# Weight splits off GpSimd, finer waits before scores and the output projection, and in seven of sixteen Runge-Kutta stages the square of q on ScalarE

## The chip, the cores and the metric

One core of one Trainium2 chip runs the whole kernel. The metric is the device time of one execution in microseconds (us), taken as the median over runs; lower is better. Engines are named PE (TensorE), DVE (VectorE), ACT (ScalarE), POOL (GpSimd) and SP (SyncE, which issues the transfers).

## The reference

Inputs are x (32 x 32 x 256) and a condition of 32 x 256. Two blocks follow each other.

- First block: `x = x + minGRU(DiT(x, cond))`. DiT is a layer norm with a condition-dependent scale and shift, attention with 16 heads of 128 over 32 tokens, a gated output projection and residual, a second such norm and a GELU MLP of width 1024. minGRU is a gated linear recurrence over the 32 tokens.
- Second block: `x = x + FFN(scan(cond, x))`. The scan runs 32 time steps, each a classical Runge-Kutta step of four stages; FFN is a block-sparse MLP that keeps 4 of 16 hidden blocks for each row. The scan's derivative is what the change touches most:

```python
def _derivative(q, p, drive, coupling, bias):
    i_couple = jnp.tanh(q) @ coupling.T
    dq = q - q ** 3 / 3.0 - p + drive + i_couple + bias
    dp = EPSILON * (q + ALPHA - BETA * p)
    return (dq, dp)
```

Step t needs the result of step t-1, so its 32 x 4 = 128 stages form one chain.

## The kernel before

Every engine has its program written out by hand, with semaphores between them; nothing is scheduled by a planner. Matrix products run in fp16 in three parts: an operand is split into a high part (fp16 of 16 times the value) and a low part (what is left), and high x high, high x low and low x high are summed.

**Start and four attention passes.** The layer norm and `x1` come first (`drive`, then `x1_pair`). Then four passes of four heads each (`for i in range(NQUAD)`). In a pass PE runs, for heads j = 0 to 3, `project(j)` (q and k), `values`, `scores(j)`, `mix(j)` (probabilities times values) and `out_project`, through five PSUM banks; a bank used again waits until DVE has emptied it. ACT copies each bank to its high part (`high`), DVE subtracts to the low part and frees the bank (`low_proj`, `low_values`, `low_pv`), DVE adds the output projections into `acc` (`add_heads`), and DVE, ACT and POOL make the softmax and place it in block-diagonal form (`shift`, `exps`, `normalise`, `place_high`, `place_low`). Eight pieces of weights per pass are split: ACT writes the high part (L528), POOL scales the weights in place (L473) and subtracts (L475), and SP loads the next pass's piece when that is done (`split_ready`).

**Waits on PE in a pass.** `taken(use)` waits until a bank has been emptied. `scores(j)` (L850) waits for both the last projections' banks before its first product; `out_project` with c = 0 (L883) waits for both halves of each head's `mix`.

**The last pass and the middle.** In the last pass ACT and POOL also split the first eight pieces of MLP weights (L550, then POOL L464 and L466). DVE gates the heads and adds the residual (`close_heads`, L1201 and L1203, three of four before `low_pv(3)`), adds the last heads (`last_heads`, L1212 and L1215), takes mean and variance (`token_var`) and finishes the square root that ACT begins (`root_x2` on ACT, `token_scale` on DVE). Then `modulate`, `x1_low`, and PE's `hidden_layer(0)`, `output_layer(0)`, `hidden_layer(1)`, `gates(0)`, `output_layer(1)`, `gates(1)`, with the minGRU on DVE.

**The scan.** 32 steps in eight groups of four, so a group has 16 stages, numbered `at` = 0 to 15. A stage is

1. ACT: `th16` = tanh(q) in fp16 (L754), then `th32` = tanh(q) in fp32 (L755), then scalings of p or pieces of the FFN (L732, L740, L745);
2. DVE: `sq` = q*q (L1499), `cub` = (sq + c)*q (L1505), `thlo` = th32 - th16 (L1495, which waits for th32), `base` (L1511), and running sums for later stages (`lin` L1603, `pacc` L1613) between them;
3. PE: the drive, then th16 x two coupling parts (8 matmuls), then thlo x one coupling part (4 matmuls), then pieces of the previous group's FFN (`FILL`);
4. DVE: `qs` or `qn` = score*h + base (L1517), which starts the next stage.

`group_work(n, at, slot)` puts DVE's share of the FFN into slot 0 (behind thlo) or slot 1 (before L1517): `split_h` (L1543), the top-4 selection, `split_q` (L1587) and `put_out` (L1552, from the third group on). In a stage whose `at` is a multiple of 4 (s = 0), thlo stands ahead of cub.

## Time and profile before

| | us |
|---|---|
| median of 3 runs | 533.71 (532.94 to 535.42) |
| the profiled execution | 534.34 |
| its span, first to last instruction | 532.6 |
| start and first pass, to 81.4 | 81.4 |
| second and third pass | 57.35 and 56.95 |
| last pass and its end, 195.7 to 273 | 77.3 |
| MLP and minGRU, 273 to 343.7 | 70.7 |
| scan, 343.7 to 521 | 177.3 |
| end, 521 to 532.6 | 11.6 |

Over the span PE is busy 454.7 us, DVE 418.1, ACT 319.1 and POOL 179.6. A share of busy time is an average over very different parts: in the scan DVE is busy 174.05 of 177.30 us, in the third pass 36.22 of 56.95. A busy time on DVE includes the latency of an instruction, and the next one may start before it ends, so the distances between starts say more than the busy times.

### The profile page before, as it was taken

How to read it: one execution, taken by the hardware profiler on the slowest of the kernel's cores; microseconds unless marked ns; L12 is line 12 of the kernel's file. 1: busy time of each engine (PE TensorE's matmuls, PEld its weight loads, DVE VectorE, ACT ScalarE, POOL GpSimd, SP SyncE). 2: the span in 40 equal slices, each digit the busy share in tenths (PEclk: the TensorE clock that was granted, in tenths of full speed). 3: DMA queues.
4: the chain of work that ended last, by engine and by line, in shares of the span. 5: the costliest groups of instructions: out<-in, count | busy, mean ns of one | idle time of the engine just before them, and what ended most of it. 6: DMA issues, size and time to landing. Idle time of an engine off the chain costs nothing.

```text
span 532.6 us, 13455 instructions
## 1 busy us (share of the span) xinstructions
PE 454.7 (85%) x4832; PEld 312.3 (59%) x4832; DVE 418.1 (79%) x1632; ACT 319.1 (60%) x881; POOL 179.6 (34%) x173
## 2 busy tenths in 40 slices
PE   2999789998999989987569998398887888879886
PEld 2555576456655665556425443286776767767676
DVE  4968765668566666577886786999999999999994
ACT  1377763787477746896258763555656556565563
POOL 4528347563737363879800890000000000000000
PEclk9899899999999999999769999777979788797799
DMA  8961502020112000000000000000000000000000
GB/s 304 414 268 38 124 1 80 17 62 1 24 55 62 17 0 0 0 1 0 0 0 1 1 2 0 0 4 1 0 1 12 1 10 10 0 10 1 10 10 21
DMA packets 10127, 20.82 MB, mean 39 GB/s; under 512 B 1456, under 2 KB 4720, under 8 KB 9456
## 3 DMA queue, kind: packets, MB, share of 16 engines
q1 hardware_dynamic: 9536, 19.89, 11.1%
q10 hardware_dynamic: 560, 0.60, 0.3%
q8 instruction: 10, 0.16, 0.1%
q14 instruction: 21, 0.17, 0.1%
HBM read 19.40 MB, written 1.08 MB: 38 GB/s over the span
## 4 chain that ended last, share of the span: by engine, by line
DVE 47%; PE 33%; ACT 10%; issue 6%; DMA 1%; POOL 1%; SPq 0%; DVEq 0%; ACTq 0%
PE bank L791 26%; DVE base L1511 5%; PE score L791 5%; DVE lin L1603 5%; DVE qs L1517 4%; DVE cub L1505 3%; DVE big L1284 3%; DVE sq L1499 3%; DVE pacc L1613 2%; ACT sraw L586 2%; ACT ao_sb L561 1%; DVE thlo L1495 1%; DVE ao_sb L1284 1%; DVE big L1543 1%; DMA ao_sb<-xtok 1%
## 5 line engine op out<-in xcount | busy, mean ns | idle before, releaser
L791 PE MATMUL bank<-x,pairs_store 128*128 128x512 f16 x384 | 87.8, 386 | 0.0
L482 POOL TENSOR_TENSOR ptx<-pt,ptx 32x256 f16<-32x256 f32 x64 | 42.8, 668 | 71.0 <-ACT ptx L593 67.3
L791 PE MATMUL score<-th,coup_part 128*128 128x32 f16 x1024 | 48.1, 182 | 18.9 <-ACT th L754 16.3
L791 PEld LDWEIGHTS bank<-x,pairs_store 128*128 128x128 f16 x384 | 37.9, 100 | 44.3 <-issue 3.0
L561 ACT ACTIVATE big<-bank,pass_b 128x512 f16<-128x512 f32 x64 | 42.8, 685 | 28.5 <-PE bank L791 26.5
L791 PE MATMUL bank<-pairs_store,ao_sb 128*128 128x256 f16 x384 | 48.6, 283 | 10.5 <-DVE ao_sb L1284 9.9
L791 PEld LDWEIGHTS score<-th,coup_part 128*128 128x128 f16 x1024 | 36.4, 100 | 30.4 <-ACT th L754 29.1
L754 ACT ACTIVATE th<-qs 128x64 f16<-128x64 f32 x96 | 24.4, 254 | 49.7 <-DVE qs L1517 49.7
L1284 DVE SCALAR_TENSOR_TENSOR big<-bank,pass_b,big 128x512 f16<-128x512 f32 x64 | 44.9, 741 | 11.6 <-ACT big L561 11.6
L791 PEld LDWEIGHTS bank<-pairs_store,ao_sb 128*128 128x128 f16 x384 | 37.5, 101 | 19.4 <-DVE ao_sb L1284 10.2
L791 PE MATMUL bank<-pairs_store,x 128*128 128x512 f16 x192 | 43.4, 379 | 0.0
L791 PE MATMUL score<-drive_pair,scaled_eye 128*128 x256 | 32.3, 209 | 11.9 <-DVE drive_pair L1446 8.9
L791 PE MATMUL bank<-big,f_sb 128*128 128x128 f16 x456 | 39.8, 232 | 0.2 <-DVE big L1543 0.2
L791 PE MATMUL bank<-q_high,f_sb 128*128 128x128 f16 x288 | 39.3, 251 | 0.0
L791 PE MATMUL score<-thlo,coup_part 128*128 128x32 f16 x512 | 34.8, 183 | 3.6
L791 PEld LDWEIGHTS score<-drive_pair,scaled_eye 128*128 128x128 f16 x256 | 25.2, 120 | 14.2 <-issue 13.9
L791 PE MATMUL bank<-q_low,f_sb 128*128 128x128 f16 x144 | 33.5, 252 | 0.0
L1282 DVE TENSOR_TENSOR big<-bank,big 128x512 f16<-128x512 f32 x32 | 21.5, 682 | 14.4 <-ACT big L559 14.4
L473 POOL TENSOR_SCALAR wqk_sb<-wqk_sb 128x512 f32<-128x512 f32 x16 | 23.8, 1489 | 23.8 <-ACT pairs_store L528 23.1
L791 PE MATMUL score<-big 128*128 128x128 f16 x384 | 25.2, 224 | 7.6 <-DVE big L1284 7.6
L791 PEld LDWEIGHTS bank<-pairs_store,x 128*128 128x128 f16 x192 | 18.6, 98 | 21.7
L732 ACT ACTIVATE pscaled<-ps 128x64 f32<-128x64 f32 x160 | 29.9, 243 | 0.4 <-DVE ps L1621 0.4
(196 smaller groups left out, 1133.1 us busy)
## 6 DMA issues: line engine op xcount, KB each, us to landing
wqk_sb<-wqk SPq DMA_DIRECT2D x16, 256.0 KB, 2.7
wv_sb<-wv SPq DMA_DIRECT2D x4, 512.0 KB, 5.3
wo_sb<-wo SPq DMA_DIRECT2D x4, 512.0 KB, 3.7
f_sb<-ffn_w SPq DMA_DIRECT2D x2, 1024.0 KB, 14.4
ao_sb<-xtok SPq DMA_DIRECT2D x4, 256.0 KB, 5.6
big<-ada_w SPq DMA_DIRECT2D x1, 1024.0 KB, 9.1
x_sb<-xT SPq DMA_DIRECT2D x1, 1024.0 KB, 13.1
w_sb<-w1T SPq DMA_DIRECT2D x1, 1024.0 KB, 16.8
```

The source lines that it names most:

```text
L473: nc.gpsimd.tensor_scalar(w, w, WSCALE, None, ALU.mult).then_inc(pool_scaled, 1)
L482: nc.gpsimd.tensor_tensor(ptx[s, 1, :, s], pt[s], ptx[s, 0, :, s], ALU.subtract).then_inc(ptx_ready, 1)
L561: ins = nc.scalar.activation(dst, src, ACT.Identity, bias=bias)
L732: nc.scalar.activation(pscaled[:, j], ps[:], ACT.Copy, scale=PSCALE[j]).then_inc(p_scaled, 1)
L754: nc.scalar.activation(th16[:], src, ACT.Tanh).then_inc(th16_ready, 1)
L791: return nc.tensor.matmul(dst, lhsT, rhs, start=start, stop=stop, **kw)
L1282: ins = V.tensor_tensor(lo, bank[bank_of(use)][:], hi, ALU.subtract)
L1284: ins = V.scalar_tensor_tensor(lo, bank[bank_of(use)][:], bias, hi, ALU.add, ALU.subtract)
L1499: squared = mark(V.tensor_tensor(kb(sq[:]), q, q, ALU.mult))
L1511: based = mark(stt(base[:], cub[:], -STAGE_H[s] / 3.0, linear, ALU.mult, ALU.add))
L1517: stt(qs[:, s] if s < 3 else qn[:], kb(score[:, s % 2, 0:KB * B]), STAGE_H[s] / CSCALE, kb(base[:]), ALU.mult, ALU.add).then_inc(q_ready, 1)
L1603: lined[n] = mark(stt(kb(lin[:, n]), q, row, src, ALU.mult, ALU.add))
```

## The change

1. **Splits.** POOL no longer splits weights. DVE writes each low part in one instruction, `w*16 - high`, with nothing scaled in place: piece 0 ahead of the first `drive` products, pieces 1 to 3 behind `x1`, then in each pass pieces 4 to 7 among the low parts and pieces 0 to 3 of the next pass between the last `add_heads`. The 16 MLP pieces go to DVE too: 0 to 3 ahead of `shift(3)` in the last pass, 4 to 7 and 12 to 15 among the hidden layer's low parts, 8 to 11 before `residual(0)`. POOL keeps `place_low`.
2. **Waits on PE.** `scores(j)` waits for its first two banks before product 0 and for the other two before product 4. `out_project` waits for the first half of `mix` at c = 0 and for the second at c = 2.
3. **Second norm.** `close_heads(2)` moves behind `token_scale(0)`, `close_heads(3)` behind `x1_low(0)`. The root of the second half is made by DVE alone (an integer seed and three Newton steps); ACT takes one root and loads the GELU table at once.
4. **Scan.** In the stages 7, 9, 10, 11, 13, 14 and 15 of each group ACT squares q behind th32, DVE's `sq` goes, and DVE runs thlo and the FFN piece ahead of cub.

```diff
+        SQUARE_AT = (7, 9, 10, 11, 13, 14, 15)
...
-                for t in range(NSPLIT):
-                    split(t)
-                    if t == 3:
...
+                place_low(0)
+                pool.wait_ge(ptx_ready, i * (QUAD * NB4) + NB4)
...
+            act.wait_ge(tok_var_ready, 1 + G // 2)
+            nc.scalar.activation(tok_std[:, 0:G // 2], tok_mv[:, 0:G // 2, 1], ACT.Sqrt, bias=eps[:]).then_inc(tok_std_ready, 1)
+            nc.scalar.activation(eps_gelu[:], eps[:], ACT.Gelu)
...
                     nc.scalar.activation(th32[:], src, ACT.Tanh).then_inc(th32_ready, 1)
+                    if n in SQUARE_AT:
+                        nc.scalar.activation(square_q[:], src, ACT.Square).then_inc(squared_ready, 1)
...
                 def scores(j):
-                    taken(USE_PROJ[j] + 2)
-                    taken(USE_PROJ[j] + 3)
...
                     for g in range(G):
+                        if g % 4 == 0:
+                            taken(USE_PROJ[j] + g // 2)
+                            taken(USE_PROJ[j] + g // 2 + 1)
...
+                    if c % 2 == 0:
+                        for j in js:
+                            taken(USE_PV[j] + c // 2)
...
+                def low_weights(i, *ts):
+                    for t in ts:
+                        w, pair = split_arrays(*SPLIT_ORDER[t])
+                        dve.wait_ge(w_high_ready, i * NSPLIT + t + 1)
+                        V.scalar_tensor_tensor(pair[:, 1], w, WSCALE, pair[:, 0], ALU.mult, ALU.subtract
+                                               ).then_inc(split_ready, 1)
...
                 low_pv(1)
+                if i == NQUAD - 1:
+                    mlp_lows(0, 1, 2, 3)
                 shift(3)
...
                     for c in range(KB * NH):
+                        low_weights(i + 1, c)
                         add_heads(1, c)
...
-                squared = mark(V.tensor_tensor(kb(sq[:]), q, q, ALU.mult))
+                at = 4 * (t % UNROLL) + s
+                by_act = at in SQUARE_AT
+                if not by_act:
+                    squared = mark(V.tensor_tensor(kb(sq[:]), q, q, ALU.mult))
                 if second:
                     second()
                 if late:
                     low(t, s)
-                dve.wait_ge(dve_step, squared)
-                cubed = mark(stt(kb(cub[:]), kb(sq[:]), -3.0 - 3.0 * own_q / STAGE_H[s], q, ALU.add, ALU.mult))
-                if not late:
+                if by_act:
+                    group_work(t // UNROLL, at, 0)
+                    low(t, s)
+                    group_work(t // UNROLL, at, 1)
+                    dve.wait_ge(squared_ready, len(SQUARE_AT) * (t // UNROLL) + SQUARE_AT.index(at) + 1)
+                else:
+                    dve.wait_ge(dve_step, squared)
+                cubed = mark(stt(kb(cub[:]), kb((square_q if by_act else sq)[:]), -3.0 - 3.0 * own_q / STAGE_H[s], q,
+                                 ALU.add, ALU.mult))
+                if not late and not by_act:
                     low(t, s)
                 ready()
-                group_work(t // UNROLL, 4 * (t % UNROLL) + s, 0)
+                if not by_act:
+                    group_work(t // UNROLL, at, 0)
                 dve.wait_ge(dve_step, cubed)
                 based = mark(stt(base[:], cub[:], -STAGE_H[s] / 3.0, linear, ALU.mult, ALU.add))
                 if third:
                     third()
-                group_work(t // UNROLL, 4 * (t % UNROLL) + s, 1)
+                if not by_act:
+                    group_work(t // UNROLL, at, 1)
```

How the order on DVE moves in stage 10, a scan stage with a `put_out`. Names: `lin` are the running sums, `x<-bank,drive` is the `put_out`, `square_q` is ACT's square. Before:

```order
L1603 SCALAR_TENSOR_TENSOR lin<-qs,lin 128x64
L1499 TENSOR_TENSOR sq<-qs 128x64
L1603 SCALAR_TENSOR_TENSOR lin<-qs,lin 128x64
L1505 SCALAR_TENSOR_TENSOR cub<-sq,qs 128x64
L1495 TENSOR_TENSOR thlo<-th 128x64
L1511 SCALAR_TENSOR_TENSOR base<-cub,lin 128x64
L1603 SCALAR_TENSOR_TENSOR lin<-qs,lin 128x64
L1552 SCALAR_TENSOR_TENSOR x<-bank,drive 128x128
L1517 SCALAR_TENSOR_TENSOR qs<-score,base 128x64
```

The same stage in the changed kernel:

```order
L1641 SCALAR_TENSOR_TENSOR lin<-qs,lin 128x64 x2
L1521 TENSOR_TENSOR thlo<-th 128x64
L1590 SCALAR_TENSOR_TENSOR x<-bank,drive 128x128
L1540 SCALAR_TENSOR_TENSOR cub<-square_q,qs 128x64
L1548 SCALAR_TENSOR_TENSOR base<-cub,lin 128x64
L1641 SCALAR_TENSOR_TENSOR lin<-qs,lin 128x64
L1555 SCALAR_TENSOR_TENSOR qs<-score,base 128x64
```

Before, cub stands ahead of thlo and the FFN piece last, between base and qs. Now thlo and the piece stand ahead of cub, and cub, base, lin and qs follow them.

The end of the last pass on DVE, before, from the second half of `add_heads` to the variance. L1201 and L1203 are `close_heads`, L1284 is `low_pv(3)`, L1212 and L1215 `last_heads`:

```order
L1332 TENSOR_TENSOR acc<-bank,acc 128x512
L1201 TENSOR_TENSOR acc<-acc,drive 128x512
L1203 TENSOR_TENSOR acc<-acc,centred 128x512
L1201 TENSOR_TENSOR acc<-acc,drive 128x512
L1203 TENSOR_TENSOR acc<-acc,centred 128x512
L1201 TENSOR_TENSOR acc<-acc,drive 128x512
L1203 TENSOR_TENSOR acc<-acc,square 128x512
L1284 SCALAR_TENSOR_TENSOR ao_sb<-bank,pass_b,ao_sb 128x512 x2
L1212 TENSOR_TENSOR nn_<-bank,drive 128x512
```

The same place in the changed kernel (L1187 and L1189 are `close_heads`, L1283 `low_pv(3)`):

```order
L1338 TENSOR_TENSOR acc<-bank,acc 128x512
L1187 TENSOR_TENSOR acc<-acc,drive 128x512
L1189 TENSOR_TENSOR acc<-acc,centred 128x512
L1187 TENSOR_TENSOR acc<-acc,drive 128x512
L1189 TENSOR_TENSOR acc<-acc,centred 128x512
L1283 SCALAR_TENSOR_TENSOR ao_sb<-bank,pass_b,ao_sb 128x512 x2
L1198 TENSOR_TENSOR nn_<-bank,drive 128x512
```

One `close_heads` of three has left the place ahead of `low_pv(3)`.

## Rows read from the trace of the kernel before

**Rows 1.** Stretches: us, busy per engine (instructions), granted PE clock, DMA share, GB/s
```profile
343.70:521.00 177.30, 151.54 (x2657) 127.52 (x2657) 174.05 (x1168) 101.11 (x467) 0.00 (x0) 0.84 0.02 5
```
**Rows 2.** Timeline, one stage (14) of the sixth group: start, us, engine, line, tiles
```profile
451.29 0.23 DVE L1517 SCALAR_TENSOR_TENSOR qs<-score,base 128x64 f32<-128x64 f32 x1
...
451.71 0.24 ACT L755 ACTIVATE th<-qs 128x64 f32<-128x64 f32 x1
...
451.99 0.23 DVE L1495 TENSOR_TENSOR thlo<-th 128x64 f16<-128x64 f32 x1
...
452.27 0.26 PE L791 MATMUL score<-thlo,coup_part 128*128 128x32 f16 x4
...
452.64 0.23 DVE L1517 SCALAR_TENSOR_TENSOR qs<-score,base 128x64 f32<-128x64 f32 x1
```
**Rows 3.** Timeline, DVE, stage 9 with its put_out
```profile
444.33 0.22 DVE L1517 SCALAR_TENSOR_TENSOR qs<-score,base 128x64 f32<-128x64 f32 x1
...
445.47 0.37 DVE L1552 SCALAR_TENSOR_TENSOR x<-bank,drive 128x128 f32<-128x128 f32 x1
445.76 0.22 DVE L1517 SCALAR_TENSOR_TENSOR qs<-score,base 128x64 f32<-128x64 f32 x1
```
**Rows 4.** Timeline, DVE, a stage with at = 0: thlo to cub to base
```profile
432.56 0.23 DVE L1495 TENSOR_TENSOR thlo<-th 128x64 f16<-128x64 f32 x1
432.71 0.22 DVE L1505 SCALAR_TENSOR_TENSOR cub<-sq,q_group 128x64 f32<-128x64 f32 x1
...
432.98 0.22 DVE L1511 SCALAR_TENSOR_TENSOR base<-cub,pscaled 128x64 f32<-128x64 f32 x1
```
**Rows 5.** Timeline, DVE: a 128-wide piece to qs; base to qs with nothing between
```profile
457.94 0.28 DVE L1587 TENSOR_TENSOR q_low<-q_group,q_high 128x128 f16<-128x128 f32 x1
458.17 0.23 DVE L1517 SCALAR_TENSOR_TENSOR qs<-score,base 128x64 f32<-128x64 f32 x1
...
466.14 0.23 DVE L1511 SCALAR_TENSOR_TENSOR base<-cub,pscaled 128x64 f32<-128x64 f32 x1
466.40 0.22 DVE L1517 SCALAR_TENSOR_TENSOR qs<-score,base 128x64 f32<-128x64 f32 x1
```
**Rows 6.** Waits of PE in the second and third pass: us in total, times, longest
```profile
PE score L791 <- DVE big L1284: 3.9, 4, 1.3
PE bank L791 <- DVE ao_sb L1284: 3.0, 4, 1.1
```
**Rows 7.** Timeline, end of the third pass
```profile
188.03 2.87 POOL L482 TENSOR_TENSOR ptx<-pt,ptx 32x256 f16<-32x256 f32 x4 [3.62 <-ACT ptx L593]
...
194.12 4.39 PE L791 MATMUL bank<-pairs_store,ao_sb 128*128 128x256 f16 x36 [0.35 <-DVE ao_sb L1284]
```
**Rows 8.** Timeline, end of the last pass and the second norm
```profile
242.45 0.42 DVE L1295 TENSOR_REDUCE smax<-sraw 128x8 f32<-128x256 f32 x1 [2.62 <-ACT sraw L586]
...
251.47 1.65 DVE L1201 TENSOR_TENSOR acc<-acc,drive 128x512 f32<-128x512 f32 x1
...
254.06 1.40 DVE L1284 SCALAR_TENSOR_TENSOR ao_sb<-bank,pass_b,ao_sb 128x512 f16<-128x512 f32 x2
255.60 6.98 PE L791 MATMUL bank<-pairs_store,ao_sb 128*128 128x256 f16 x36 [3.46 <-DVE ao_sb L1284]
...
273.16 13.21 PE L791 MATMUL bank<-x,wqk_sb 128*128 128x512 f16 x48 [4.97 <-issue]
```
**Rows 9.** L1201 in all (ns min/median/max), then DVE groups, 247.8 to 263: busy us, mean ns
```profile
L1201 DVE TENSOR_TENSOR acc<-acc,drive x4: 684/992/1651, 247.8 to 265.5; 128x512 f32<-128x512 f32 x4
...
L1203 DVE TENSOR_TENSOR acc<-acc,centred 128x512 f32<-128x512 f32 x2 | 1.7, 868 | 0.1
L1215 DVE TENSOR_TENSOR acc<-acc,tn 128x512 f32<-128x512 f32 x1 | 1.7, 1660 | 0.1
...
L1215 DVE TENSOR_TENSOR acc<-acc,nn_ 128x512 f32<-128x512 f32 x1 | 1.2, 1204 | 0.1
```
**Rows 10.** Timeline, ACT's switch to another table before the MLP
```profile
275.99 1.28 ACT L680 ACT_TABLE_LOAD   x1
```

More of the change, by code:

```diff
@@ L19 @@
 BF16 = mybir.dt.bfloat16
+I32 = mybir.dt.int32
+ROOT_SEED = 0x5F3759DF
 AX_X = mybir.AxisListType.X
@@ L678, in _ @@
             x1_high(NH)
-            root_x2(1)
-            nc.scalar.activation(eps_log[:], eps[:], ACT.Gelu)
             for h in range(NH):
@@ L1168, in _ @@
                 last.then_inc(x1_ready, 1)
+            first_low_weights(1, 2, 3)
             def late_start():
@@ L1184, in _, with mlp_lows @@
             ln = Own(dve, ln_step)
+            def mlp_lows(*ts):
+                for t in ts:
+                    w, high_part, low_part = mlp_arrays(t)
+                    dve.wait_ge(mlp_high_ready, t + 1)
+                    V.scalar_tensor_tensor(low_part, w, WSCALE, high_part, ALU.mult, ALU.subtract).then_inc(mlp_split, 1)
             def pair_of(c):
@@ L1228, in token_scale @@
                 gs = slice(h * G // 2, (h + 1) * G // 2)
-                dve.wait_ge(tok_std_ready, h + 2)
-                ln.step(V.reciprocal(tok_rstd[:, gs], tok_std[:, gs]))
-                ln.wait()
-                ln.step(V.tensor_tensor(tok_tmp[:, gs], tok_rstd[:, gs], tok_rstd[:, gs], ALU.mult))
-                ln.wait()
-                ln.step(V.scalar_tensor_tensor(tok_tmp[:, gs], tok_mv[:, gs, 1], LN_EPS, tok_tmp[:, gs], ALU.add, ALU.mult))
-                ln.wait()
-                ln.step(V.tensor_scalar(tok_tmp[:, gs], tok_tmp[:, gs], -0.5, 1.5, ALU.mult, ALU.add))
-                ln.wait()
-                ln.step(V.tensor_tensor(tok_rstd[:, gs], tok_tmp[:, gs], tok_rstd[:, gs], ALU.mult))
+                if h == 0:
+                    dve.wait_ge(tok_std_ready, 2)
+                    ln.step(V.reciprocal(tok_rstd[:, gs], tok_std[:, gs]))
+                    steps = 1
+                else:
+                    dve.wait_ge(tok_var_ready, 1 + G)
+                    ln.step(V.tensor_scalar(tok_std[:, gs], tok_mv[:, gs, 1], LN_EPS, None, ALU.add))
+                    ln.wait()
+                    ln.step(V.tensor_scalar(tok_tmp[:, gs].bitcast(I32), tok_std[:, gs].bitcast(I32), 1, None,
+                                            ALU.arith_shift_right))
+                    ln.wait()
+                    ln.step(V.tensor_scalar(tok_rstd[:, gs].bitcast(I32), tok_tmp[:, gs].bitcast(I32), -1, ROOT_SEED,
+                                            ALU.mult, ALU.add))
+                    steps = 3
+                for _ in range(steps):
+                    ln.wait()
+                    ln.step(V.tensor_tensor(tok_tmp[:, gs], tok_rstd[:, gs], tok_rstd[:, gs], ALU.mult))
+                    ln.wait()
+                    ln.step(V.scalar_tensor_tensor(tok_tmp[:, gs], tok_mv[:, gs, 1], LN_EPS, tok_tmp[:, gs], ALU.add, ALU.mult))
+                    ln.wait()
+                    ln.step(V.tensor_scalar(tok_tmp[:, gs], tok_tmp[:, gs], -0.5, 1.5, ALU.mult, ALU.add))
+                    ln.wait()
+                    ln.step(V.tensor_tensor(tok_rstd[:, gs], tok_tmp[:, gs], tok_rstd[:, gs], ALU.mult))
                 ln.wait()
@@ L1316, in low_projs @@
                         low_proj(j, k)
+                def low_weights(i, *ts):
+                    for t in ts:
+                        w, pair = split_arrays(*SPLIT_ORDER[t])
+                        dve.wait_ge(w_high_ready, i * NSPLIT + t + 1)
+                        V.scalar_tensor_tensor(pair[:, 1], w, WSCALE, pair[:, 0], ALU.mult, ALU.subtract
+                                               ).then_inc(split_ready, 1)
                 def low_values(*gs):
@@ L1338, in _ @@
                 normalise(0)
-                low_values(3, 4, 5)
-                low_projs(1)
+                low_values(3, 4)
+                low_weights(i, 4)
+                low_values(5)
+                low_proj(1, 0)
+                low_proj(1, 1)
+                low_weights(i, 5)
+                low_proj(1, 2)
+                low_proj(1, 3)
+                low_weights(i, 6)
                 if i == 0:
@@ L1345, in _ @@
                 normalise(1)
-                low_projs(2)
+                low_proj(2, 0)
+                low_proj(2, 1)
+                low_weights(i, 7)
+                low_proj(2, 2)
+                low_proj(2, 3)
                 low_pv(0)
@@ L1361, in _ @@
                     for c in range(KB * NH):
+                        low_weights(i + 1, c)
                         add_heads(1, c)
                 else:
-                    for c in range(3):
-                        close_heads(c)
+                    close_heads(0)
+                    close_heads(1)
                     low_pv(3)
@@ L1371, in _ @@
                     token_scale(0)
-                    close_heads(3)
+                    close_heads(2)
                     last_heads(2)
@@ L1378, in _ @@
             x1_low(0)
+            close_heads(3)
             last_heads(3)
```

49 lines of the change are left out of this document (13 added, 36 removed).

## Prediction

> **What bounds the kernel now.** I read the stretches first, then the timeline of single stages, then PE's waits, then the end of the last pass. The sum is made against the profiled execution, 534.34 us, which is 0.6 above the median of 533.71.
>
> The scan takes 177.3 of 532.6 us, and DVE is busy 174.05 of it [rows 1]; a stage lasts 177.3 / 128 = 1.39 us. The timeline shows why the busy share alone says little. In stage 14 q comes at 451.29, th32 runs on ACT from 451.71 to 451.95, thlo starts on DVE at 451.99, its matmuls on PE at 452.27 (0.26 long), and the next q at 452.64, 0.11 behind their end [rows 2]. That is a closed loop of 1.35 us, q to th32 to thlo to PE to q. In it thlo cannot start before q + 0.70, because it waits for th32, whatever DVE does. DVE fills the same 1.35 us with sq, cub, base and sums, most of them in the 0.70 us ahead of thlo. So the stage has two chains of nearly the same length, and the question is what stands ahead of thlo and what behind it.
>
> In the second and third pass PE waits 3.9 + 3.0 = 6.9 us on DVE [rows 6], 3.5 a pass. From the last pass to the MLP, PE sits idle 3.46 us before 255.60, and `hidden_layer(0)` starts at 273.16 [rows 8]. From there PE runs nearly without a break to 334, so what moves that start moves the rest.
>
> **The scan: 56 stages.** Removed: sq on DVE. Added: a square on ACT behind th32. An ACT instruction of this size takes 0.24, as th32 does [rows 2]; it starts some 0.15 behind th32's start, so it ends at q + 0.42 + 0.15 + 0.24 = 0.81. ACT's later pieces in these stages move by 0.15, and have the rest of the stage as cover; without it the next th16 would be late by as much.
>
> Moved: cub now comes behind thlo and the FFN piece. None of the seven stages has a piece in slot 0, so between the sums and thlo DVE has nothing to do: thlo stays at q + 0.70, and the slot that sq leaves is idle time. Behind thlo a chain begins that formerly ran ahead of it:
>
> - thlo to the FFN piece: +0.15 (thlo to cub, 432.56 to 432.71 [rows 4]);
> - a 128-wide piece to cub: +0.20 (0.23 to qs with one more wait instruction between [rows 5]; 0.03 off for that);
> - cub to base: +0.27 (432.71 to 432.98 [rows 4]), since base reads cub;
> - base to q: between 0.26 with nothing in between [rows 5] and 0.32 with a `lin` of 0.14 and two waits; taken 0.29.
>
> Sum: 0.70 + 0.15 + 0.20 + 0.27 + 0.29 = 1.61 against 1.35, so +0.26 in stages 7, 11, 13, 14 and 15. The square, ready at 0.81, is waited for by nobody, and the coupling on PE, ready at 1.24, isn't either: the FFN piece, cub and base end last. Bounds per stage: +0.18 (the shortest of each distance, a piece of 0.17) and +0.33 (a longer base to q, an extra wait instruction at cub).
>
> Stages 9 and 10 carry a `put_out`, 0.29 to the next instruction, and last 1.43 now (444.33 to 445.76 [rows 3]). After: 0.70 + 0.15 + 0.29 + 0.27 + 0.29 = 1.70, +0.27. In the first two groups they have no `put_out`: 0.70 + 0.15 + 0.27 + 0.29 = 1.41 against 1.35, +0.06.
>
> Over the scan: 5 x 8 x 0.26 = 10.4, 2 x 6 x 0.27 = 3.2, 2 x 2 x 0.06 = 0.2: **+13.8 us**, between +9.5 and +17.
>
> **The passes.** DVE takes 8 splits a pass at 0.69 each (an instruction of 128x512 with two SBUF inputs, minimum 0.684 [rows 9]), 5.5 us. Most lie where DVE waits for ACT. Three places are on PE's path. (1) Piece 7 stands ahead of the last two `low_proj(2)`: it takes back what the finer wait at `scores(2)` gives. (2) `scores(3)` starts some 0.7 sooner, but ACT's copy of the scores is queued behind `place_high(2)`, and `mix(3)` waits for the last ptx, made on POOL from 188.03 to 190.90 after a wait on ACT of 3.62 [rows 7]. The wait moves ahead of `mix(3)` and stays. (3) Piece 0 of the next pass stands ahead of the `add_heads` whose bank PE needs: +0.69, less the 0.35 before 194.12 [rows 7] that the finer wait saves: +0.3. For three pass ends +0.9. In the first pass three early pieces stand behind x1, and three more among late work: +0.4. Bounds: -3 (half of PE's waits gone) and +4 (piece 0 in full, and one split a pass more on the path).
>
> **The end of the last pass.** `close_heads(2)` leaves the path: 251.47 to 254.06, -2.6 [rows 8]. DVE no longer meets POOL's scalings: L1201 0.992 twice and L1203 0.868 twice against 0.684, L1215 1.66 and 1.20 against 0.69 [rows 9]: 0.62 + 0.37 + 0.97 + 0.51 = -2.5. Against it, MLP pieces 0 to 3 ahead of `shift(3)`: 4 x 0.69 = 2.76 in a wait of 2.62 [rows 8], and some 0.4 for meeting POOL's ptx there: +0.55. Together **-4.6**. Bounds: -7 (PE at full clock in `hidden_layer(0)`, which takes 13.21 for the 48 matmuls [rows 8]) and -2.
>
> The Trainium skill's SBUF — State Buffer (the section that explains the port diagram) says that DVE and GpSimd share one port pair as an exclusive lock, and that the loser blocks for the whole instruction. By it each of the four pieces could wait for a whole ptx instruction of 0.72, 2.9 us in place of 0.4, and the time would be 2.5 higher. L1201's average excess of 0.31 to 0.97 is nearer to a part of an instruction.
>
> Priced at nothing: the two table loads (ACT then runs ahead of PE's first hidden tile; if uncovered 1.3 [rows 10]); the DVE square root of the second half, ten small instructions of 0.2 under 13.21 us of PE, and if late, `turn_normed(1)` is late; MLP pieces 4 to 15 under PE's matmuls; the next weights' loads, many us ahead.
>
> **Sum.** 534.34 + 13.8 + 0.9 + 0.4 - 4.6 = 544.8; on the scale of the medians **544.2 us**.
>
> **The rivals.**
>
> 1. *The scan is a count of DVE's instructions, and one less is a gain* (ends on the other side). For it: DVE busy at 98%, and stages with `put_out` last longer. Then each of 56 stages loses one slot of 0.135, -7.6, and with the front's -3.3 the time is 522.8. It decides if thlo can start before q + 0.70 or the piece and cub fit beside it. Against it: thlo starts 0.04 behind th32's end [rows 2] with sq in place or not. Chance 0.05.
> 2. *PE's waits in the passes really vanish* (half of 3.5 or more in four passes, and a full clock at the MLP, -9 in all beyond mine): 535. ptx [rows 7] speaks against it. Chance 0.06.
> 3. *The passes become bound by DVE*: one or two splits a pass more on the path, 4 x 1.2: 549. Chance 0.08.
> 4. *ACT must load tables for Square*. One load takes 1.28 [rows 10]; two per stage, 112 x 1.28 = 143: 687. The built program has no load near the squares. Chance 0.01. The Trainium skill, ScalarE: Activation LUTs (Table sets), says that functions come in sets, that a switch costs about 2.66 us, and doesn't name square under the GELU set; by its figure it would be twice that.
> 5. The forecast, 0.80.
>
> **How the numbers follow.** A measurement tells 0.5%, about 2.7 us, from no change: same is 531.0 to 536.4. Faster is rival 1 and a small part of 2: 0.07. Same is most of 2 and the cheap ends of mine (9.5 with -8 in front gives 535): 0.06. Slower 0.87. The range takes the scan's +9.5 with -6 in front, 537, to +17 with -1.5, 549, and so most of rival 3.
>
> **What would show it.** In the changed kernel's seven stages: thlo at q + 0.70, the piece 0.15 behind it, cub 0.2 behind that, and base to q without a wait on PE; DVE's busy time in the scan lower although the scan is longer; PE's wait for ACT's th16 longer in these stages. Scan about 191 us, `hidden_layer(0)` at about 270 us. Wrong would be: thlo ahead of q + 0.6, these stages at 1.4 or less, or passes off 57 us by more than 1.

## The result, and the profile after

The changed kernel takes 539.22 us (median of 5 runs, 538.80 to 541.05) against 533.90 (5 runs beside it): the ratio is 1.0097, 95% interval 1.0069 to 1.0126. It is slower by about 1%. The forecast was 544.2 us, range 537 to 549, with 0.87 on slower; so 10.5 us were forecast over the 533.71 of the record, and 5.3 came. The profiled execution is the slowest of the five, 541.05 us, span 539.3.

First the stretches of the changed kernel: start, us, busy time of PE, PE's weight loads, DVE, ACT, POOL (instructions), granted PE clock, DMA share, GB/s.

```profile
334.34:527.20 192.86, 160.06 (x2667) 133.85 (x2668) 174.84 (x1119) 109.60 (x523) 0.00 (x0) 0.77 0.02 5
133.46:190.32 56.86, 53.14 (x432) 34.03 (x432) 40.59 (x76) 38.52 (x77) 10.95 (x16) 1.00 0.12 37
```

The first line runs 2 us past the last q. From the first scan matmul to the end of the last q, DVE is busy 173.76 of 176.98 us before (1166 instructions) and 173.25 of 191.04 in the changed kernel (1110). So 14 us were added, and 56 squares less took only 0.5 us off DVE's busy time, because instructions that stand further apart overlap less: in the run e3 below, which has all 1166 in the new order, they cover 178.99 us. The busy share fell from 98% to 91%, and the stage is still DVE's to end. The third pass (second line) has DVE busy 40.59 us where it was 36.22, and takes no longer.

One stage of the seven, at = 14, in the timeline (start, us, engine, line, tiles, idle time before and its releaser):

```profile
425.57 0.22 DVE L1555 SCALAR_TENSOR_TENSOR qs<-score,base 128x64 f32<-128x64 f32 x1
...
426.13 0.24 ACT L722 ACTIVATE square_q<-qs 128x64 f32<-128x64 f32 x1
...
426.25 0.22 DVE L1521 TENSOR_TENSOR thlo<-th 128x64 f16<-128x64 f32 x1 [0.20 <-ACT th L720]
426.39 0.28 DVE L1581 TENSOR_TENSOR big<-big 128x128 f16<-128x128 f32 x1
426.53 0.29 PE L758 MATMUL score<-thlo,coup_part 128*128 128x32 f16 x4
426.60 0.22 DVE L1540 SCALAR_TENSOR_TENSOR cub<-square_q,qs 128x64 f32<-128x64 f32 x1
...
426.92 0.23 DVE L1548 SCALAR_TENSOR_TENSOR base<-cub,lin 128x64 f32<-128x64 f32 x1
427.06 0.22 DVE L1641 SCALAR_TENSOR_TENSOR lin<-qs,lin 128x64 f32<-128x64 f32 x1
427.20 0.22 DVE L1555 SCALAR_TENSOR_TENSOR qs<-score,base 128x64 f32<-128x64 f32 x1
```

Read it against [rows 2]. thlo still starts 0.68 behind q, now with 0.20 of idle time ahead of it. Behind it come the FFN piece (+0.14), cub (+0.21), base (+0.32), a running sum and the next q (+0.28): 1.63 us instead of 1.35. PE's coupling is done at 426.82, 0.38 ahead of q; before it was 0.11 ahead.

Stage 9, with a `put_out`, on DVE alone, against [rows 3]:

```profile
417.36 0.22 DVE L1555 SCALAR_TENSOR_TENSOR qs<-score,base 128x64 f32<-128x64 f32 x1
...
418.06 0.22 DVE L1521 TENSOR_TENSOR thlo<-th 128x64 f16<-128x64 f32 x1 [0.21 <-ACT th L720]
418.20 0.36 DVE L1590 SCALAR_TENSOR_TENSOR x<-bank,drive 128x128 f32<-128x128 f32 x1
418.48 0.22 DVE L1540 SCALAR_TENSOR_TENSOR cub<-square_q,qs 128x64 f32<-128x64 f32 x1
418.80 0.23 DVE L1548 SCALAR_TENSOR_TENSOR base<-cub,lin 128x64 f32<-128x64 f32 x1
...
419.08 0.22 DVE L1555 SCALAR_TENSOR_TENSOR qs<-score,base 128x64 f32<-128x64 f32 x1
```

Outside the scan, the edge of a pass against [rows 7]:

```profile
127.15 1.48 PE L758 MATMUL bank<-pairs_store,ao_sb 128*128 128x256 f16 x12 [1.30 <-DVE ao_sb L1283]
129.32 1.51 PE L758 MATMUL bank<-ptx,big 128*128 128x128 f16 x24 [0.69 <-POOL ptx L470]
...
134.29 1.91 PE L758 MATMUL bank<-pairs_store,ao_sb 128*128 128x256 f16 x16 [0.83 <-DVE acc L1338]
```

The wait on POOL's ptx has moved ahead of the mix (0.69), and the last line shows a new one: 0.83 us for DVE's addition, behind the next pass's first weight piece.

To compare many runs I cut each profiled execution at PE's instructions: first projection, first projection of each later pass, first FFN matmul, first matmul of the scan, and DVE's last q. In us:

| kernel | to first projection | first pass | second, third pass | last pass and its end | MLP, minGRU | scan | behind it |
|---|---|---|---|---|---|---|---|
| before | 21.9 | 62.1 | 57.3, 57.0 | 74.8 | 70.6 | 176.8 | 12.1 |
| before, scan part added (e2) | 22.4 | 59.7 | 57.3, 57.0 | 73.3 | 70.4 | 191.4 | 15.2 |
| changed | 20.8 | 59.3 | 56.9, 56.9 | 69.6 | 71.0 | 190.8 | 14.1 |
| changed, scan part undone (e1) | 19.7 | 58.8 | 56.9, 56.9 | 69.4 | 70.9 | 177.0 | 13.7 |

The first two run the same program as far as the scan, and so do the last two. Within each pair the difference is the scatter of one execution: up to 1.1 us to the first projection, 2.4 in the first pass, 1.5 in the last, next to nothing in between.

### The profile page after: what moved, and what is told of

It is laid out like the page before. It is cut to its first block, busy times and chain, and to the rows that moved or that the text cites. A ratio compares the mean times of both kernels' runs of the same rounds, so it can differ in the third digit from the quotient of the medians.

```text
span 539.3 us, 13473 instructions
## 1 busy us (share of the span) xinstructions
PE 458.9 (85%) x4832; PEld 317.9 (59%) x4832; DVE 431.0 (80%) x1634; ACT 327.2 (61%) x936; POOL 48.7 (9%) x77
## 4 chain that ended last, share of the span: by engine, by line
DVE 43%; PE 33%; ACT 13%; issue 6%; POOL 2%; DMA 1%; DVEq 0%; ACTq 0%
PE bank L758 29%; DVE lin L1641 4%; DVE pacc L1651 3%; DVE base L1548 3%; DVE cub L1540 3%; DVE thlo L1521 3%; DVE qs L1555 3%; DVE big L1283 2%; PE score L758 2%; POOL ptx L470 2%; ACT th L720 2%; ACT sraw L557 2%; DVE big L1581 2%; ACT ptx L564 2%; PE spare L758 2%
## 5 line engine op out<-in xcount | busy, mean ns | idle before, releaser
L470 POOL TENSOR_TENSOR ptx<-pt,ptx 32x256 f16<-32x256 f32 x64 | 44.8, 700 | 195.4 <-ACT ptx L564 191.8
L758 PE MATMUL bank<-pairs_store,ao_sb 128*128 128x256 f16 x384 | 46.1, 275 | 9.7 <-DVE ao_sb L1283 6.4
L1283 DVE SCALAR_TENSOR_TENSOR big<-bank,pass_b,big 128x512 f16<-128x512 f32 x64 | 45.1, 738 | 9.2 <-ACT big L532 9.1
L758 PE MATMUL bank<-big,f_sb 128*128 128x128 f16 x456 | 46.5, 258 | 0.2 <-DVE big L1581 0.2
L758 PE MATMUL bank<-q_high,f_sb 128*128 128x128 f16 x288 | 37.4, 243 | 0.0
L758 PEld LDWEIGHTS bank<-big,f_sb 128*128 128x128 f16 x456 | 34.2, 115 | 0.5 <-issue 0.3
L1521 DVE TENSOR_TENSOR thlo<-th 128x64 f16<-128x64 f32 x128 | 28.7, 225 | 6.9 <-ACT th L720 6.7
L758 PE MATMUL bank<-q_low,f_sb 128*128 128x128 f16 x144 | 32.1, 245 | 0.0
L758 PEld LDWEIGHTS score<-thlo,coup_part 128*128 128x128 f16 x512 | 22.2, 101 | 14.3
```

Of the source, the lines that this page charges most:

```text
L470: nc.gpsimd.tensor_tensor(ptx[s, 1, :, s], pt[s], ptx[s, 0, :, s], ALU.subtract).then_inc(ptx_ready, 1)
L758: return nc.tensor.matmul(dst, lhsT, rhs, start=start, stop=stop, **kw)
L1283: ins = V.scalar_tensor_tensor(lo, bank[bank_of(use)][:], bias, hi, ALU.add, ALU.subtract)
L1521: V.tensor_tensor(thlo[:], th32[:], th16[:], ALU.subtract).then_inc(lo_ready, 1)
```

## The experiments

### The scan part, taken out and put in alone

`e1_scan_undone` is the changed kernel with

```
-        SQUARE_AT = (7, 9, 10, 11, 13, 14, 15)
+        SQUARE_AT = ()
```

> The changed kernel with an empty list of stages for ScalarE's square, so every stage runs as before; the rest of the change (low parts on VectorE, the order at the pass edges, the finer TensorE waits) stays. Theory A (the seven stages cost the time and nothing else in the scan changed; the part ahead of the scan gained 9.4 us by its first matmul, 343.73 to 334.34): scan back from about 193 to 178.7 us, first scan matmul unchanged at 334.3, median 539.2 - 14.1 = 525, so 0.983 of the kernel before. Rival B (part of the stages' cost belongs to the fewer POOL operations or to another part of the change): scan stays above 181, median above 528.

Measured: 524.92 us (524.41 to 526.71, 5 runs), ratio to before 0.9855, 0.9831 to 0.9879. `e2_scan_alone` is the kernel before with ScalarE's square and the new order of these stages, nothing else.

> The kernel before with only the scan part of the change. Theory A (the parts are additive, the seven stages alone cost 14 us): first scan matmul at 343.7 as before, scan 192.9, median 533.9 + 14.1 = 548, so 1.026. Rival B (the stages' cost depends on how the rest was rearranged): less than 1.02.

Measured: 549.28 us, ratio 1.0307, 1.0268 to 1.0347. Both ways the seven stages cost 14 to 16 us by the medians, and the scan went from 177 to 191 us (e2's profile also has 15.2 us behind the scan, see the last section). Theory A holds. It also follows that the rest of the change gains some 8 us, and that the version without the scan part is faster than either kernel.

### What in the stage costs the time

`e3_vector_square` keeps the change's order, but VectorE squares:

```
-                if not by_act:
-                    squared = mark(V.tensor_tensor(kb(sq[:]), q, q, ALU.mult))
+                squared = mark(V.tensor_tensor(kb(sq[:]), q, q, ALU.mult))
```

> The changed kernel, but in the seven stages VectorE squares q itself (0.13 us in the idle time while it waits for tanh), in the change's order otherwise: low part of tanh with the FFN piece around it, then the cube. Theory A (what costs is the place of the cube behind the low part, which waits for tanh, and the low part's latency; who squares doesn't matter): stages stay at 1.63 and 1.67 to 1.72 us, scan 192 to 194, median 538 to 540.5. Rival C (the cube waits for ScalarE's square, which lands behind ScalarE's second copy of tanh at 0.80): each of the seven stages gets back 0.1 us or more, scan 187 or less, median 534 or less.

Measured: 539.85 us, ratio 1.0127, 1.0103 to 1.0151; scan 191.0 us. DVE's stage 14:

```profile
425.61 0.22 DVE L1550 SCALAR_TENSOR_TENSOR qs<-score,base 128x64 f32<-128x64 f32 x1
...
425.88 0.22 DVE L1525 TENSOR_TENSOR sq<-qs 128x64 f32<-128x64 f32 x1
...
426.30 0.23 DVE L1519 TENSOR_TENSOR thlo<-th 128x64 f16<-128x64 f32 x1
426.44 0.28 DVE L1576 TENSOR_TENSOR big<-big 128x128 f16<-128x128 f32 x1
426.64 0.22 DVE L1535 SCALAR_TENSOR_TENSOR cub<-sq,qs 128x64 f32<-128x64 f32 x1
...
427.24 0.22 DVE L1550 SCALAR_TENSOR_TENSOR qs<-score,base 128x64 f32<-128x64 f32 x1
```

sq takes the idle slot ahead of thlo, and the stage lasts 1.63 as in the change. Moving the square to ScalarE by itself bought and cost nothing: the order on DVE, with the FFN piece and the cube behind thlo, is the whole cost.

`e4_piece_first` takes the FFN piece out of the chain:

```
                     group_work(t // UNROLL, at, 0)
+                    group_work(t // UNROLL, at, 1)
                     low(t, s)
-                    group_work(t // UNROLL, at, 1)
```

> The changed kernel, but in the seven stages both halves of the FFN piece run ahead of the low part of tanh, in the idle time while VectorE waits for tanh; ScalarE squares as in the change. Theory A (a stage is the sum along VectorE's chain from the arrival of tanh on: low part, piece, cube, base, so a piece moved out of it gives its length back, 0.15 us, and with the copy to the output some 0.25): stages 1.43 to 1.50, scan about 181 to 184, median 527 to 531. Rival D (a piece in the idle time delays the low part, and the wait moves on to TensorE, whose last matmuls of the stage then end it): stages above 1.55, scan above 187, median above 533.

Measured: 531.55 us (10 runs), ratio 0.9972, 0.9945 to 0.9998; scan 183.0 us. The scan is as theory A says, the median 0.5 above its 531, and a part of D is right. Stage 14 follows A:

```profile
422.20 0.22 DVE L1555 SCALAR_TENSOR_TENSOR qs<-score,base 128x64 f32<-128x64 f32 x1
...
422.61 0.28 DVE L1581 TENSOR_TENSOR big<-big 128x128 f16<-128x128 f32 x1
...
422.89 0.23 DVE L1521 TENSOR_TENSOR thlo<-th 128x64 f16<-128x64 f32 x1
423.03 0.23 DVE L1540 SCALAR_TENSOR_TENSOR cub<-square_q,qs 128x64 f32<-128x64 f32 x1
...
423.64 0.22 DVE L1555 SCALAR_TENSOR_TENSOR qs<-score,base 128x64 f32<-128x64 f32 x1
```

It lasts 1.44, which is 0.69 + 0.14 + 0.33 + 0.28: the chain from tanh on without the piece. In stages 7, 11 and 15, where the running sum `pacc` comes late, the piece does delay thlo:

```profile
418.17 0.23 DVE L1651 SCALAR_TENSOR_TENSOR pacc<-qs,pacc 128x64 f32<-128x64 f32 x1
418.31 0.28 DVE L1581 TENSOR_TENSOR big<-big 128x128 f16<-128x128 f32 x1
418.52 0.22 DVE L1521 TENSOR_TENSOR thlo<-th 128x64 f16<-128x64 f32 x1
```

Here q was at 417.72, so thlo starts at +0.80 instead of +0.69, and the stage lasts 1.53. DVE still ends it, 0.17 us or more behind the coupling on PE, and not TensorE as D has it. With the cube ahead of tanh, as before, there are 1.34 to 1.35 us in both stages.

### Waits and the order at the middle, undone one by one

The base is now e1 (524.9 us). `e5_coarse_waits` puts PE's waits back:

```
-                    if c % 2 == 0:
+                    if c == 0:
                         for j in js:
-                            taken(USE_PV[j] + c // 2)
-                    if c == 0:
+                            taken(USE_PV[j])
+                            taken(USE_PV[j] + 1)
```

This is in `out_project`; and `scores(j)` waits again for the last projections' banks ahead of its first product.

> The kernel with the scan part undone (median 524.9), and in it TensorE's finer waits for heads and value groups put back to the coarse ones of the kernel before. Theory E (the finer waits pay for the weight pieces that VectorE took over: the idle gaps per pass are 3.5 us before and 3.6 after, although VectorE has eight more pieces): each of the four passes grows by 0.4 to 1.2 us, median 526.5 to 529.5. Rival F (the pieces of weights sit in slots where nothing waited, and the finer waits are worth nothing): within 0.5 us of 524.9.

Measured: 529.43 us, ratio 0.9921, 0.9897 to 0.9945. The first pass takes 61.6 instead of 58.8, the second and third 57.66 instead of 56.87, the last 70.3 instead of 69.4. Theory E, and the median even reaches the upper end of its range: the finer waits are worth 4.5 us, and without them a pass is 0.3 to 0.7 us longer than in the kernel before, since DVE's eight pieces are in it.

`e6_old_norm_order` closes the first three groups of heads together again and gives the second half's root back to ScalarE:

```
-                    close_heads(0)
-                    close_heads(1)
+                    for c in range(3):
+                        close_heads(c)
```

> The kernel with the scan part undone, and in it the second norm as before: heads 0 to 2 closed together ahead of the last one, ScalarE taking the roots of the second half only when all heads are closed. From the end of the third pass to the first FFN matmul the time was 79.0 us before (194.12 to 273.16) and is 72.0 in this base (189.59 to 261.57). Theory G (my forecast's split: 2.6 us of the 7.0 come from the order of the closing heads, the rest from the weights' low parts that no longer run on POOL): 74.0 to 75.2 us, median 527 to 528.5. Rival H (the order is worth nothing, the gap at the turned norm is filled by something else): within 0.5 us of 72.0 and of 524.9. Rival I (the order is all of it): 78.5 us, median 531.5.

Measured: 524.98 us, ratio 0.9827, 0.9799 to 0.9855. The stretch that the text names took 72.8 us instead of 72.0, and the next one gave 0.6 back (70.3 for 70.9). The median is rival H's; the 0.8 is a little more than H allows and far from G's 2 to 3.2. The three groups of heads, from the first to the instruction that PE waits for:

```profile
243.60 0.80 DVE L1193 TENSOR_TENSOR acc<-acc,drive 128x512 f32<-128x512 f32 x1
...
248.05 1.40 DVE L1289 SCALAR_TENSOR_TENSOR ao_sb<-bank,pass_b,ao_sb 128x512 f16<-128x512 f32 x2
```

They take 4.45 us. In the kernel before the same six instructions took 6.22, to the 254.06 of [rows 8]:

```profile
247.84 0.89 DVE L1201 TENSOR_TENSOR acc<-acc,drive 128x512 f32<-128x512 f32 x1
```

So 1.8 us of the 6.22 were the stretching of these instructions by POOL, and 1.3 of the 1.8 stand in the third group, 2.59 us before and 1.32 here. That group is `close_heads(2)`, whose whole 2.6 us the forecast gave to its move. The move by itself is worth 0.8 us up to the first FFN matmul, and nothing that the medians show.

### POOL's instructions, put back without their effect

`e7_pool_busy`: POOL scales and subtracts again, 37 times where the kernel before did it 48 times, on two scratch tiles.

```
+            def busy():
+                own.step(nc.gpsimd.tensor_scalar(idle_out[:], idle_in[:], WSCALE, None, ALU.mult))
+                own.wait()
+                own.step(nc.gpsimd.tensor_tensor(idle_out[:], idle_in[:], idle_out[:], ALU.subtract))
+                own.wait()
...
+                busy_split(i, 0, 1, 2, 3)
                 place_low(0)
```

> The kernel with the scan part undone, and POOL again does a scaling and a subtraction of 128x512 for each piece of weights at the place where it did them before, but on two scratch tiles that nobody reads (for the MLP's weights pieces 0 to 4 only, to the start of the FFN). Nothing waits for them but POOL's own placing of the low parts. Theory J (the front was faster than I had forecast because VectorE and POOL no longer share time: the contention that I had put at 2.5 us in the last pass is larger and also acts in the start and in each pass): first pass edge from 75.9 to 77.5 or more, the last pass 1.5 us or more longer than 72.0, median 528 to 533. Rival K (POOL's operations slow nobody, the gain came from the chain of waits alone): median within 0.7 us of 524.9 and VectorE's mean for one 32x256 placing or 128x512 scaled subtraction unchanged.

Measured: 538.82 us, ratio 1.0093, 1.0056 to 1.0130. That is 14 us over its base, more than any theory had. Against e1's row it is 2.4 to the first projection, 8.3 in the first pass (67.1), 1.55 in each of the next two (58.4) and 1.8 in the last (71.2), less 1.7 behind the scan. Rival K is out. Theory J has the place right and the size too small. DVE in the start, in e1, without POOL's instructions:

```profile
11.59 0.17 DVE L1101 TENSOR_SCALAR tok_tmp<-tok_tmp 128x8 f32<-128x8 f32 x1
...
12.00 2.68 DVE L1106 TENSOR_SCALAR ao_sb<-ao_sb,tok_mv,tok_rstd 128x256 f32<-128x256 f32 x8
...
20.73 1.28 DVE L1139 TENSOR_TENSOR drive<-drive,ada 128x512 f32<-128x512 f32 x2
```

and in the kernel before, with them:

```profile
11.35 0.57 DVE L1133 TENSOR_SCALAR tok_tmp<-tok_tmp 128x8 f32<-128x8 f32 x1
...
12.15 3.95 DVE L1138 TENSOR_SCALAR ao_sb<-ao_sb,tok_mv,tok_rstd 128x256 f32<-128x256 f32 x8
...
21.56 2.24 DVE L1161 TENSOR_TENSOR drive<-drive,ada 128x512 f32<-128x512 f32 x2
```

In e7 they take 0.57, 4.06 and 2.35 us. So the same three rows have nearly the same lengths in the two kernels where POOL is at work, and shorter ones where it isn't. In the kernel before the excess is 2.6 us together, in the stretch that leads to the first projections. In e7 DVE's own weight pieces, which the kernel before does not have, lengthen too: 0.68 us alone, up to 1.75 beside POOL, while its instructions that read a PSUM bank stay at 0.65 to 0.69 and 0.71 to 0.75.

The excess follows a rule that the trace shows. Two places in the kernel before, beside the 251.47 1.65 of [rows 8]:

```profile
251.24 1.33 POOL L466 TENSOR_TENSOR wqk_sb<-f_sb,wqk_sb 128x512 f16<-128x512 f32 x1
...
260.49 1.15 POOL L466 TENSOR_TENSOR wo_sb<-f_sb,wv_sb 128x512 f16<-128x512 f32 x1
260.53 1.66 DVE L1215 TENSOR_TENSOR acc<-acc,tn 128x512 f32<-128x512 f32 x1
```

POOL's subtractions end at 252.57 and 261.64. DVE's instructions, which take 0.68 alone, start inside them and end at 253.12 and 262.19: 0.55 behind POOL's end both times, so each waited for what was left of POOL's instruction and then ran at its own length. Up to the scan, the fourteen profiles have 106 DVE instructions of the kinds `tensor_scalar`, `tensor_tensor` and `scalar_tensor_tensor`, none of them reading PSUM and all with a counterpart in e1, that started inside a POOL subtraction (its ptx ones too) with more than 0.3 us of it left. All 106 were lengthened, to 0.12 to 0.15 us less than their own length behind POOL's end. Of 294 that read PSUM there, none was. POOL's scalings lengthened a part of such instructions, and by 0.42 us at most.

In the first pass POOL's placing of ptx also stands behind its own useless pieces, so e7 bounds the contention in this layout from above and does not measure it alone. What e7 shows there: PE waits 4.8 us (twice) at a bank for DVE's `big` in the first pass, where e1 has 0.2.

`e10_pool_no_scaling` is the converse: the kernel before, with POOL's 48 scalings left out, so that the low parts of the weights are not the right ones.

```
-                    nc.gpsimd.tensor_scalar(w, w, WSCALE, None, ALU.mult).then_inc(pool_scaled, 1)
-                    pool.wait_ge(pool_scaled, i * NSPLIT + t + 1)
                     nc.gpsimd.tensor_tensor(pair[:, 1], w, pair[:, 0], ALU.subtract).then_inc(split_ready, 1)
```

> The kernel before, without POOL's scaling ahead of each subtraction of the weights' low parts: this scaling is left out, 48 instructions of 1.49 to 1.73 us, and the low parts of the weights are then not the reference's. Everything else, VectorE's work above all, is as before. Theory J (POOL's instructions on weights lengthen VectorE's between on-chip tiles, and that sat on the chain in the start, in each pass and at the end of the last one): about half of the overlap goes, VectorE's small 128x8 instruction in the start that took 0.57 instead of 0.17, the two of 128x512 that took 2.24 together instead of 1.28 and the 1.43 us score subtraction come back in part, first scan matmul 3 to 7 us earlier than 343.7, median 526 to 530. Rival K (before's chain does not feel POOL): median within 1 us of 533.

Measured: 527.41 us, ratio 0.9895, 0.9862 to 0.9929; the first matmul of the scan at 336.85, 6.9 us earlier. The first pass takes 58.3 us against 62.1 and 59.7, the second and third 56.97 as before or 0.3 less, the last 73.4 against 74.8 and 73.3. Theory J: POOL's work on weights did sit on the chain of the kernel before, and most of that in the start and the first pass. The small instruction of the start now takes 1.11 us, since it meets a subtraction (11.58 to 12.73) and not a scaling, and the normalisation behind it 2.67 instead of 3.95.

### The edge of a pass

The base is e1 again. `e8_edge_moved` subtracts the next pass's first four pieces behind all additions:

```
                     for c in range(KB * NH):
-                        low_weights(i + 1, c)
                         add_heads(1, c)
+                    low_weights(i + 1, 0, 1, 2, 3)
```

> The kernel with the scan part undone, and at the three pass edges all four pieces of the next pass's weights are subtracted behind all four additions of heads, not one ahead of each. Theory L (the 0.83 us that TensorE waits at each edge for the first accumulated head is the length of the piece ahead of it, 0.7): that gap falls to 0.2, the next pass's first projection has its pieces in time since TensorE has some 10 us of other work, 0.5 to 0.7 us less per edge, median 522.8 to 523.6. Rival M (the pieces come too late and the next pass's first projections wait for them, or TensorE waits at the later heads instead): median 525 or more.

Measured: 528.14 us, ratio 0.9890, 0.9851 to 0.9929, so 3 us worse than its base, with 57.81 us a pass for 56.87. Rival M:

```profile
134.11 2.78 PE L758 MATMUL bank<-pairs_store,ao_sb 128*128 128x256 f16 x24 [0.23 <-DVE acc L1338]
138.28 4.06 PE L758 MATMUL bank<-x,pairs_store 128*128 128x512 f16 x18 [1.38 <-DVE pairs_store L1321]
```

The 0.83 is gone, and 1.38 stands at the next projection, which now waits for a piece. `e9_piece_behind` only swaps the two lines of the loop.

> The kernel with the scan part undone, and at the pass edges each piece of the next pass's weights behind the addition of heads that it stood ahead of (the run with all four behind all four additions lost 0.9 us per pass: the edge's 0.83 us gap went, and TensorE waited 1.38 us at the next pass's first projection instead). Theory L2 (the first projection has slack for 0.7 us but not for four pieces): the 0.84 us gap falls to 0.2 or less, no new wait over 0.3, median 522.8 to 524. Rival M2 (the first projection waits at once for the pieces as well): passes of 56.87 us stay or grow, median 524.5 to 526.

Measured: 522.71 us (521.30 to 524.22, 6 runs), ratio 0.9796, 0.9763 to 0.9830. Theory L2:

```profile
133.04 2.78 PE L758 MATMUL bank<-pairs_store,ao_sb 128*128 128x256 f16 x24 [0.23 <-DVE acc L1338]
135.66 5.34 PE L758 MATMUL bank<-x,pairs_store 128*128 128x512 f16 x24
```

No second wait; the passes take 56.25 instead of 56.87. This is the fastest version found, with e11 and e12 level.

### Two more orders, without a gain

`e11_mlp_piece_later` is e9 with one of the four MLP pieces moved:

```
-                    mlp_lows(0, 1, 2, 3)
+                    mlp_lows(0, 1, 2)
...
                 low_pv(2)
+                if i == NQUAD - 1:
+                    mlp_lows(3)
```

> The run with the pieces behind the additions at the pass edges (median 522.7), and in the last pass only three of the MLP's first four pieces ahead of shift(3), the fourth behind low_pv(2). The forecast priced the four at +0.55 against a wait of 2.62. In that run they take 3.83 us, one of them stretched beside POOL's ptx, and shift(3) starts at 236.51, 0.75 behind ScalarE's last sraw at 235.75. Theory N (shift(3) is late by these 0.75 and TensorE's wait at 240.76 with it): shift(3) follows sraw by 0.05, the 2.45 us wait falls to 1.8, the first FFN matmul comes 0.5 to 0.8 earlier, median 522.0 to 522.5. Rival O (the wait is set by another chain, or the moved piece stands on the path itself): start of the first FFN matmul unchanged within 0.2.

Measured: 522.96 us, ratio 0.9786, 0.9759 to 0.9814. shift(3) started at 235.97 and the wait fell from 2.45 to 1.85 as theory N says, and the next one, 1.03 in e9, took it back. The first FFN matmul starts at 260.79 for 260.84, so in the end it is rival O:

```profile
240.23 1.48 PE L758 MATMUL bank<-pairs_store,ao_sb 128*128 128x256 f16 x12 [1.85 <-DVE ao_sb L1283]
243.21 1.51 PE L758 MATMUL bank<-ptx,big 128*128 128x128 f16 x24 [1.50 <-POOL ptx L470]
```

`e12_values_ahead` is e11 with `low_pv(2)` ahead of `add_heads(0, 1)` in all four passes.

> The same kernel, and in all four passes low_pv(2) ahead of add_heads(0, 1) instead of behind it. TensorE's largest gap per pass is 1.30 us at the out projection, released by VectorE's ao_sb, whose instruction stands behind this 0.58 us addition. Theory P (VectorE's order there sets TensorE): the gap falls to 0.7, passes from 56.25 to 55.7, median 520 to 521. Rival Q (the low part waits for ScalarE's high part or for the bank of values anyway, or TensorE then waits for the bank that the addition frees): passes unchanged within 0.1 us.

Measured: 523.42 us, ratio 0.9798, 0.9771 to 0.9826; passes of 56.25 as before. Rival Q, in its second form:

```profile
124.06 0.83 PE L758 MATMUL bank<-pairs_store,ao_sb 128*128 128x256 f16 x6 [0.69 <-DVE ao_sb L1283]
125.32 0.83 PE L758 MATMUL bank<-pairs_store,ao_sb 128*128 128x256 f16 x6 [0.43 <-DVE acc L1338]
126.83 1.51 PE L758 MATMUL bank<-ptx,big 128*128 128x128 f16 x24 [0.68 <-POOL ptx L470]
```

The 1.30 splits into 0.69 and 0.43 (for the bank that the addition frees), and ptx comes last either way.

## Why the forecast was right, and where it was off

**The scan, +13.8: right.** The table has +14.1 (176.8 to 190.8). By its terms, for a stage like 14: thlo at 0.68 to 0.70 (0.70), to the piece 0.14 (0.15), to cub 0.20 (0.20), to base 0.32 (0.27), to q 0.28 (0.29). The sum is 1.63 against 1.61. The one term outside rounding is cub to base: in these stages a wait instruction of DVE's own starts 0.26 behind cub, and base 0.07 behind it, where base followed cub by 0.27 in [rows 4]. Stage 13 came to 1.68 (1.61), from 1.40 and not 1.35. Stages 9 and 10 came to 1.72 and 1.71 (1.70), and 1.46 and 1.44 without `put_out` (1.41). Over the 56 stages the growth is 15.3 us, 1.5 more than forecast; the other 72 became 1.3 us shorter, which I had not foreseen. Half of that, 0.7, is in the seven stages with at = 0 that follow another group: 1.46 us on average before, 1.37 in the changed kernel. One of them before, whose q is at 431.87 and whose stage ends at 433.31:

```profile
432.49 0.33 PE L791 MATMUL score<-drive_pair,scaled_eye 128*128 x2 [0.38 <-issue]
```

PE's drive products start 0.60 to 0.78 behind q in these stages of the kernel before, and with them the products of th16, at 0.85 to 1.03. In the changed kernel, where the stage ahead is longer, the drive is at 0.06 to 0.22 and th16 at 0.56, as in the other stages. Why PE issues late there is open. e3 and e4 confirm the reason for the scan's growth: the order of DVE's chain, not who squares. e4 adds that the piece itself was some 8 of the 14 us.

**The second and third pass: right within 0.7.** "+0.9 for three pass ends" was -0.4 and -0.1 for two. The gaps stand where the forecast put them: ahead of the mix for ptx, and 0.83 at the edge for piece 0. What it sized too low is the finer waits, which e5 prices at 0.8 a pass.

**The end of the last pass, -4.6: right in sum, wrong in its parts.** Measured -3.7 to -5.2, by which of the two executions of the old program is taken. The term "`close_heads(2)` leaves the path, -2.6" failed: undoing it costs 0.8 there and nothing in the end (e6), for half of the 2.59 us was stretching. The stretching by POOL, put at -2.5 without that half, is larger: 1.8 between 247.84 and 254.06 (e6), and L1215's 0.51 and 0.97 [rows 9]. That the two errors cancel is luck.

**The start and the first pass, +0.4: this step failed.** Measured -4.0 from before to after, -2.0 from e2 to after. I priced the eight new pieces on DVE and did not look at DVE's own instructions in the start, though they were in the trace at 0.57 for 0.17 and 3.95 for 2.68. e10 shows the mechanism in the old kernel (-1.5 to -3.8 in the first pass with half of POOL's work), e7 in the new one, and e5 gives the finer waits 2.8 us there. How the two share the measured gain is not settled, since one execution's first pass scatters by up to 2.4.

**The total.** Ahead of the scan the forecast has -3.3 us. The profiles have -9.4 (343.73 to 334.34; `hidden_layer(0)` at 263.4, not at about 270), and the medians of e1 and its kernel before -8.2. The low end of the range took -6 there, so this part lies outside its bound. The time lies in the range since the scan came at +14 and not at its own low end, +9.5.

**The rivals.** 1 (one DVE instruction less is a gain) is out: thlo stayed at 0.69 and DVE's idle slot was filled again in e3 at no cost. 2 (PE's waits vanish) did not happen: PE still waits 1.30, 0.69 and 0.83 in a pass. 3 (passes bound by DVE) did not, though e5 shows how near it was. 4 is out: both kernels have the same number of table loads, four of 1.28 us, none of them in the scan.

**The rule of the Trainium skill** (SBUF — State Buffer, SBUF: two separate sides: of a GpSimd instruction and a VectorE one with two SBUF inputs or in a 2-port mode, the one that starts first keeps the shared port pair for the whole instruction, and the other blocks) was weighed at the four MLP pieces ahead of `shift(3)`. The trace agrees with it: see the 106 cases above. I had read it as a loss of a whole ptx instruction for each piece, 2.9 us. But a blocked instruction waits only for what is left of the other: three of the four pieces took 1.06, 1.15 and 1.15 us for 0.69, and the four took 3.81 together, 1.05 more than my 2.76 where I had put 0.4.

**Profiles and medians.** Spans of the profiled executions differ by 6.7 us, medians by 5.3; the difference is mostly the stretch behind the scan, last section.

## What to carry to other kernels

In a closed loop of engines, ask first what can run in the time in which the loop waits for another engine. An operation that needs nothing from the awaited result belongs ahead of the wait: taking it off the engine and putting its consumer behind the wait made a full engine idle and the loop longer by 0.27 us a turn. And before pricing work that moves from GpSimd to VectorE by its own instructions, compare equal VectorE instructions of the same trace inside and outside GpSimd's busy time; the excess of those on the path is what the move gives back. Here the part ahead of the scan became 8 us shorter by the medians, with 48 pieces added to VectorE and with the finer waits.

## What the runs showed of the hardware that I had not expected

- What a meeting with POOL costs a DVE instruction depends on where in POOL's instruction it starts. The 128x256 score subtraction takes 0.42 or 0.43 us in all 16 cases of e1; in the kernel before it took 1.43 once (started 0.01 behind the start of a POOL subtraction of 1.15), 0.78 once (started 0.66 behind) and 0.42 or 0.43 in the other 14. POOL pays too: beside the MLP pieces its ptx instructions took 1.00 us, where they take 0.66 alone.
- The stretch behind the scan runs the same instructions and took 12.12 us in the kernel before at a granted clock of 1.00, and 14.11 in the change at 0.83:

```profile
520.48:532.60 12.12, 8.32 (x137) 7.68 (x134) 5.19 (x25) 4.02 (x7) 0.00 (x0) 1.00 0.08 23
```

```profile
525.16:539.27 14.11, 10.36 (x135) 9.63 (x132) 5.27 (x25) 4.03 (x7) 0.00 (x0) 0.83 0.07 20
```

  It was 12.1 in e7 and e10 and 13.7 to 15.2 in the other eleven profiled kernels. The granted clock of the stretch is 1.00 in the three fast ones and 0.72 to 0.88 in the others. The profiled execution of the change has a span of 539.3 and a mean clock of 0.896, its four others spans of 537.0 to 537.6 and mean clocks of 0.898 to 0.914, so some 2 us may belong to that execution. What decides it was not tested.
- Also by the clock: PE's 36 output products that took 6.98 us in [rows 8] ran at a mean granted clock of 0.56 (0.50, the lower level of 1.2 GHz, in their first 4.6 us), behind 3.46 us without work. The same program in e2, behind the same 3.46 us, had 1.00 there and was 1.5 us shorter in the last pass.
